# Halves of the cross-attention's maxima earlier in the self-attention's steps: one TensorE group and one VectorE reduction moved in thirteen steps

## The reference, cut to what matters

```python
x = x + self_attention(layernorm(x))          # 16 heads of 8, causal, with relative positions
x = x + cross_attention(layernorm(x), ctx)    # 16 heads of 8, 77 keys, q and k normed per head
x = x + experts(layernorm(x))

# self-attention, for each sequence b of 4
logits = where(j <= i, (q @ k.T + rel[clip(j - i + 255, 0, 255)]) * 8 ** -0.5, -inf)
out = softmax(logits) @ v @ Wo + bo
# cross-attention
out = softmax(qn @ kn.T) @ v @ Wp.T + bp      # its softmax needs a maximum per token and head
```

## Time and profile before

| | us |
|---|---|
| median of three executions | 502.36 |
| the three | 502.36, 505.87, 501.76 |
| the profiled execution | 502.75 |
| span of the trace in it | 500.9 |

### The profile page before, as it was taken

How to read it: one execution, slowest core, us unless ns; L and a number is a source line. 1 busy time by engine, 2 the same in 40 slices (tenths; PEclk the granted TensorE clock), 3 DMA queues, 4 the chain that set the end, 5 groups by cost and what they waited for, 6 DMA issues and landing times.

```text
span 500.9 us, 17223 instructions
## 1 busy us (share of the span) xinstructions
PE 449.2 (90%) x7304; PEld 274.7 (55%) x7304; DVE 343.2 (69%) x692; ACT 261.3 (52%) x779; POOL 162.2 (32%) x95
## 2 busy tenths in 40 slices
PE   0758999999999799999799999989887999999997
PEld 0444565665655565655575665565445434666765
DVE  4883788646986847886847887775667587466533
ACT  1133746756556546746534655655443566554653
POOL 7235647322360672351473413075300000001000
PEclk9998999999999889999979999999898999999999
DMA  8111000000000000000000000000000005403150
GB/s 283 56 58 56 13 24 14 12 26 24 24 5 22 21 5 24 25 3 24 7 20 24 3 3 3 3 3 3 1 1 1 2 0 170 166 25 124 67 184 28
DMA packets 17465, 19.49 MB, mean 39 GB/s; under 512 B 1659, under 2 KB 14575, under 8 KB 17263
## 3 DMA queue, kind: packets, MB, share of 16 engines
q1 hardware_dynamic: 17391, 18.41, 11.3%
HBM read 16.17 MB, written 2.16 MB: 37 GB/s over the span
## 4 chain that ended last, share of the span: by engine, by line
PE 67%; DVE 20%; issue 5%; ACT 4%; DMA 2%; POOL 1%; SPq 0%; DVEq 0%; ACTq 0%; POOLq 0%
PE psT L1413 14%; PE psS L1384 13%; PE psS L1394 8%; PE psOM L1353 7%; PE psT L1773 5%; PE psS L1756 4%; DVE neg_max L1039 3%; DVE x_max L1014 2%; PE psS L1603 2%; PE psOM L1494 2%; ACT prob L653 2%; PE psT L1494 2%; PE psOM L1630 1%; DVE prob L1259 1%; DVE stage L878 1%
## 5 line engine op out<-in xcount | busy, mean ns | idle before, releaser
L653 ACT ACTIVATE prob<-psS,neg_max 128x208 f32<-128x208 f32 (+23 forms) x256 | 121.4, 480 | 73.9 <-DVE neg_max L1039 73.8
L1039 DVE TENSOR_REDUCE neg_max<-psS 128x2 f32<-128x672 f32 (+23 forms) x128 | 91.8, 717 | 64.1 <-PE psS L1394 63.2
L444 POOL TENSOR_TENSOR stat<-stat,pack_a_sb 128x4 f32<-128x4 f32 (+2 forms) x16 | 54.7, 3418 | 169.7 <-DVE stat L866 139.3
L1413 PE MATMUL psT<-pack_a_sb,prob 128*128 128x128 f32 (+4 forms) x640 | 99.0, 286 | 6.3 <-DVE pt_even L995 3.3
L1413 PEld LDWEIGHTS psT<-pack_a_sb,prob 128*128 128x128 f32 (+4 forms) x640 | 65.1, 133 | 48.4 <-issue 31.2
L1384 PE MATMUL psS<-k_v,q_both 64*32 64x336 f32 (+23 forms) x2048 | 88.4, 402 | 2.7 <-ACT prob L653 1.5
L1394 PE MATMUL psS<-rel_shifted,q_both 36*32 36x268 f32 (+16 forms) x2048 | 71.5, 337 | 0.0
L478 POOL TENSOR_TENSOR q_both<-qT,pack_a_sb 128x1024 f32<-128x1024 f32 x16 | 31.6, 1973 | 90.7 <-PE psS L1394 82.5
L1394 PEld LDWEIGHTS psS<-rel_shifted,q_both 36*32 36x32 f32 x2048 | 37.2, 109 | 24.7 <-issue 17.6
L653 ACT ACTIVATION_READ_ACCUMULATOR prob<-psS,neg_max 128x1 f32 x256 | 50.6, 197 | 0.0
L1773 PEld LDWEIGHTS psT<-pack_b_sb,prob 128*128 128x128 f32 x288 | 36.1, 191 | 18.6 <-DVE prob L1259 11.4
(11 more groups left out here) (166 smaller groups left out, 597.6 us busy)
## 6 DMA issues: line engine op xcount, KB each, us to landing
q_rep<-q_scratch SPq DMA_DIRECT2D x128, 32.0 KB
k_v<-w_scratch SPq DMA_DIRECT2D x8, 512.0 KB, 6.4
q_both<-w_scratch SPq DMA_DIRECT2D x8, 512.0 KB, 6.3
pack_b_sb<-pack_b_dram SPq DMA_DIRECT2D x1, 1641.5 KB, 10.0
X<-x_dram SPq DMA_DIRECT2D x4, 256.0 KB, 6.0
q_scratch<-qT SPq DMA_DIRECT2D x4, 256.0 KB, 2.0
out_dram<-X SPq DMA_DIRECT2D x4, 256.0 KB, 2.3
pack_a_sb<-pack_a_dram SPq DMA_DIRECT2D x1, 535.0 KB, 4.9
```

The costliest lines, as they stand in the source:

```text
L444: nc.gpsimd.tensor_tensor(st[:, 5, 0:groups], st[:, 2, 0:groups], ca["root"][0:parts, 0:groups], ALU.pow).then_inc(seeded, 1)
L653: ins = nc.scalar.activation(prob[:, s % 4, half, 0:wide], psS[:, 2 * (s % 2) + half, 0:wide], ACT.Exp, bias=neg_max[:, s % 2, half:half + 1],
L1039: v.tensor_reduce(neg_max[:, s % 2], psS[:, 2 * (s % 2):2 * (s % 2) + 2, 0:wide], AX_X, ALU.max, negate=True).then_inc(max_ready, 1)
L1413: ins = nc.tensor.transpose(psT[0:w, k % 2, at:at + T], prob[:, s % 4, half, j * T:j * T + w], ident)
```

## The change

In the thirteen steps the four matmuls of a half stand directly behind the step's scores on TensorE, with the waits of `early_probe` in front of them; before, they stood behind the transposes and behind the value multiply, if the step has one. On VectorE the reduction stands directly behind the step's `neg_max`, in front of the copies and of what the norms have in that step; before, it was the last of the step. No instruction is added or taken away, and ScalarE, GpSimd and SyncE keep their order.

```diff
@@ VectorE, in the loop over the steps
                 dve.wait_ge(scores_ready, s + 1)
                 v.tensor_reduce(neg_max[:, s % 2], psS[:, 2 * (s % 2):2 * (s % 2) + 2, 0:wide],
                                 AX_X, ALU.max, negate=True).then_inc(max_ready, 1)
+
+                if (g, u) in EARLY_PROBES:
+                    x_max_half(*divmod(EARLY_PROBES.index((g, u)), 2 * TB), psOM)
                 if s >= 2:
                     copy_units(s - 2)
...
-
-                if (g, u) in EARLY_PROBES:
-                    x_max_half(*divmod(EARLY_PROBES.index((g, u)), 2 * TB), psOM)
                 if (g, u) == EARLY_SHIFT:
@@ TensorE, in the loop over the steps
             for s in range(ALL_STEPS):
                 g, u = divmod(s, BS)
                 scores(s)
+                if (g, u) in EARLY_PROBES:
+                    early_probe(g, u)
                 if s >= 2:
                     transpose_weights(s - 2)
...
-                if (g, u) in EARLY_PROBES:
-                    early_probe(g, u)
                 if (g, u) == EARLY_SHIFT:
```

## The result

The changed kernel took 508.69 us (median of 508.75, 508.61, 508.64 and 510.57) against 502.06 for the kernel before on the same chip (502.36, 505.87, 501.76, 500.15): 1.0124 times as long, interval 1.0079 to 1.0169, 6.6 us. The forecast was 506.0 in 501.5 to 509.5. The range holds the result; the likeliest case does not, since its own range ended at 507.3. All ratios compare undisturbed runs; one execution of the kernel before, of 832.19 us, is left out of them. The profiled execution took 508.75, its span is 506.9 at a clock of 0.970 (before: 502.75, 500.9, 0.976): 6.0 us more.

What follows compares the result with a forecast made beforehand. The prediction took TensorE, busy for 90% of the span, to bound the kernel. Its terms, 0.68 + 1.06 + 0.16 + 0.45 + 1.24 = 3.59 us, added to the median of 502.36 gave 506.0 us, range 501.5 to 509.5.

Steps and rivals of the forecast that it cites:

- the likeliest case: Whole kernel: the added waits alone, without a second fall of the clock, 505.0 to 507.3 us; chance 0.40.
- The sum of the order: All thirteen steps: idle time that comes less idle time that goes, +3.59 us.
- (10, 6) and (11, 0): Half waits for `finish` in (10, 6), +0.68 us; transposes wait behind `add_y` in (11, 0), no longer hidden, +1.06.
- (13, 0) and (14, 0): Half waits for `add_y` ahead of the transposes: +0.16 us and +0.45 us.
- (14, 6) to (15, 2): `finish` and `add_y` waits delay TensorE, less 0.36 us for the value multiply's reduction in (15, 2): +1.24 us together.
- The other steps: (10, 0), (12, 0), (12, 1), (11, 6), (15, 6), (11, 1), (15, 1): what they wait for is done in time, 0.
- The hold on line 911: VectorE ahead of `add_y` at (11, 0): held until GpSimd's line 488 ends, again near 1.9 us, no gain.
- the second fall: Rival: around (15, 0) the clock falls to 0.50 too, costing 1.7 to 3.4 us, 507.7 to 509.4; chance 0.30.
- a slow stretch of (11, 0) that falls into the stall: Rival: at (11, 0) the clock falls earlier, inside the 3.7 us stall, up to 3.4 back, 502.6 to 506; chance 0.15.

Runs made afterwards that it cites:

- the two filled traces: Kernel before and changed kernel, each with spare identity transposes on TensorE in its two long stalls: 497.73 us (0.9918) and 502.25 us (0.998 of before).
- the nine alone: Kernel before with nine of the thirteen halves moved on both engines, all but (10, 6), (11, 0), (14, 6), (15, 0): 501.78 us, 1.0013.
- the step-0 kernel: Kernel before with only the halves of (11, 0) and (15, 0) moved, on both engines: 504.4 us, 1.0039.
- the old order with `head_sum` later: Kernel before with `head_sum`, which holds line 911, moved from step 7 of the third block to step 1 of the fourth: 494.58 us, 0.984.

## Why the forecast was half right

**The sum of the order was right.** 3.59 us were worked out, 3.4 measured with the clock taken out of both sides. (10, 6) and (11, 0): +1.74 forecast, +1.33 measured. By the starts in the two filled traces step 6 has 0.62 us of the 0.68, since the half starts 0.06 and not 0.11 us behind `finish`, and the scores of (11, 2) are 1.68 us later. The rest comes off behind them: in the old order, filled, the value multiply of (11, 2) had waited 0.25 us for the late reduction, which the sum had counted in (15, 2) alone, and the scores of (12, 0) had started 1.42 us behind those of (11, 7), where it is 1.18 now. (13, 0) and (14, 0): 0.61 forecast, 0.72 measured. (14, 6) to (15, 2): 1.24 forecast, 1.33 measured. The other steps: 0 forecast, and the nine alone measured 1.0013 (0.9977 to 1.0049). The terms of single halves do not simply add up, though: the step-0 kernel, with (14, 6) in its old place, takes 334.41 - 321.20 = 13.21 us from (14, 6) to (15, 3), 1.32 more than the old order (330.03 - 318.14 = 11.89), where its expectation had 0.7.

**The hold on line 911 was right.** It took 2.05 us again and ended with GpSimd's instruction, so nothing was gained by the earlier reduction. Moved out of that instruction's time, it took 0.20 us. The rule of the Trainium skill that was cited ("SBUF — State Buffer", "SBUF: two separate sides") agrees with both. The page names only some VectorE instructions for the lock, which the prediction left out. The trace of the old order with `head_sum` later fits that: within GpSimd's instruction (241.62 to 244.19) VectorE's copy out of PSUM at 242.48 took 0.69 us, as elsewhere.

**The step that failed is the clock.** The forecast gave the case with no second fall 0.40, the second fall 0.30, and 0.15 to a slow stretch of (11, 0) that falls into the stall. What came was the second fall, and the stretch of (11, 0) did not become shorter but longer: 10.2 us for 6.8. The likeness that spoke for the rival (1.85 us of idle ahead of (15, 0), 1.89 ahead of the old fall) weighed more than the 0.77 us that spoke against it. The price was off the other way: half of a stretch was put down as lost (3.4 us of 6.8), and it was less. The stretch of 6.8 us at (11, 0) costs the kernel before 2.63 us: against its filled version, one execution of each, it is 2.59 us behind at (10, 6) (241.22 less 238.63) and 5.22 at (12, 0). The two stretches of the changed kernel, 17.0 us in all, cost 6.99: against its own filled version it is 1.25 us behind at (10, 6) and 8.24 at (15, 3). So the clock's part is 6.99 - 2.63 = 4.36 us, and with the 3.38 of the order that is the 7.7 that the stage lost. The rival of the second fall gave 507.7 to 509.4 us, which holds the 508.69, but in part by luck: it had the price of a stretch too high and left out that the one at (11, 0) grew, and the two errors offset each other.

**Shown and not shown.** Shown: the four halves of step 6 and step 0 carry the loss but for 0.72 us of order at (13, 0) and (14, 0), work in their stalls gives the clock back, and the stall of (11, 0) hangs on line 911 in both orders (1.89 us to none, 3.71 to 0.80). Still open is what decides a fall. The kernel with 1.99 us of idle at (15, 0) held its clock in the execution seen, the changed kernel with 1.86 did not; and 10 us of slow stretch at (11, 0) came with the old stall as well. Runs of the kernel before spread in the same way: of 23, four had a mean clock of 0.966 and took 505.1 us on average, six had 0.976 and took 501.2. The changed kernel had 0.96 to 0.97 in all four.

## What to carry to other kernels

On the engine that bounds a kernel, an instruction that waits for another engine belongs behind the work that waits for nothing: in front of it the same wait is no longer hidden, and all that was hidden behind it comes on top. Move the two ends of a pair (the producer on one engine, the consumer on the other) together, or each engine's order makes the other wait. And count a stall of TensorE twice, once as idle time and once for the slower clock that may follow; then look for what the awaited instruction itself is held by, since moving that out of the way brought 1.6% where moving the waiter cost 1.2%.

## What the runs showed of the hardware

A small VectorE instruction can be held by GpSimd for all of its time: line 911, 128x64 elements, took 1.93, 2.05 and 1.97 us within GpSimd's 2.5 us instruction, ended together with it, and took 0.20 us elsewhere. Not every instruction was held: a copy out of PSUM took 0.69 us within GpSimd's instruction, as elsewhere.

TensorE's clock fell behind stalls and stayed at 0.50 for 3.4, 6.8 or 10.2 us, and in the stretches shown behind the two stalls TensorE was busy all the time: work did not bring it back at once. Half of the stretch was an upper bound of its price here: the 6.8 us in the kernel before cost 2.6.

The Trainium skill ("TensorE: Matmul & The Clock Gate", "HAM oscillation — how this bites in real kernels") says that waits between bursts of matmuls can put the clock back to half each time. The changed kernel's trace agrees, with a slow stretch behind each of its two long stalls. The step-0 kernel shows that it need not happen: 1.00 behind 1.99 us of idle time.

Spare transposes of an identity made kernels faster: 26 of them the kernel before by 0.8%, and 31 the changed one by 1.4% (0.998 of before, against 1.0124).
